# Seven of 392 edge gathers issued row by row on SyncE's queue, and the node-row traffic moved to ScalarE's queue

## The reference

```
xn = layernorm(x)
x  = x + relational_gnn(xn, src, dst, edge_type) + mixer(xn)
x  = x + expert_ffn(layernorm(x))          # top-1 of 32 experts per node
```

## Time and profile before

| | |
|---|---|
| median of the three runs | 785.32 us |
| the profiled execution's own time | 787.59 us |
| its span, first to last instruction | 785.8 us |
| mean granted TensorE clock | 0.904 |
| busy: PE, DVE, POOL, ACT | 76%, 49%, 58%, 21% |
| packets of SP's and ACT's DMA rows, of POOL's | 19236, 22576 |
| edge loop: first and last gather | 47.6 and 630.4 us |

### The profile page before, as it was taken

One profiled execution on the slowest core, in us unless ns is written; L12 is line 12 of the kernel. 1 busy time (PEld: TensorE's weight loads), 2 busy tenths in 40 slices (PEclk: granted clock), 3 DMA queues, 4 the chain that ended last, 5 costly groups with the idle time before them and its releaser, 6 DMA issues.

```text
span 785.8 us, 10435 instructions
## 1 busy us (share of the span) xinstructions
PE 597.3 (76%) x3180; PEld 469.0 (60%) x3181; DVE 386.4 (49%) x1272; ACT 162.6 (21%) x345; POOL 456.2 (58%) x463
## 2 busy tenths in 40 slices
PE   0367776788887884879989899898898894388970
PEld 0356565566665663767667677676676762277850
DVE  3844344333233233445557665666556576823552
ACT  0450000000000000102323222233213253144420
POOL 9146666666666666666666666766666600352264
PEclk9969997799999998699999899999999996579985
DMA  8463333333332334333344343344333416552021
GB/s 228 157 186 85 91 92 87 90 94 86 90 91 85 94 88 134 110 93 110 113 127 121 108 128 114 109 126 118 115 111 111 127 55 204 136 165 74 30 87 51
DMA packets 41872, 86.78 MB, mean 110 GB/s; under 512 B 11280, under 2 KB 23378, under 8 KB 41491
## 3 DMA queue, kind: packets, MB, share of 16 engines
q0 software_dynamic: 22576, 61.01, 26.7%
q1 hardware_dynamic: 18372, 22.95, 9.5%
q10 hardware_dynamic: 864, 2.08, 1.1%
HBM read 73.21 MB, written 12.80 MB: 109 GB/s over the span
## 4 chain that ended last, share of the span: by engine, by line
PE 38%; issue 18%; DVE 15%; another core or an unknown queue 9%; POOL 7%; DMA 6%; ACT 4%; SPq 1%; DVEq 1%; ACTq 0%; POOLq 0%
PE ps L797 18%; PE ps L845 6%; POOL gath L545 6%; DMA gath<-xn_d,src_i 3%; PE ps L1043 3%; PE ps L1052 3%; DVE wmat L1180 2%; DVE acc_raw L1207 2%; DMA both<-in_x 2%; PE ps L814 2%; PE ps L834 2%; PE ps L868 1%; DMA both<-rows_d,inv_i 1%; ACT L658 1%
## 5 line engine op out<-in xcount | busy, mean ns | idle before, releaser
L545 POOL DMA_INDIRECT gath<-xn_d,src_i x392 | 384.7, 981 | 223.7 <-issue 87.6
L797 PE MATMUL ps<-wmat,gath 128*128 128x144 f32 x1568 | 267.9, 311 | 48.1 <-DVE wmat L1180 16.1
L797 PEld LDWEIGHTS ps<-wmat,gath 128*128 128x128 f32 x1568 | 227.9, 202 | 86.4 <-issue 31.3
L1207 DVE TENSOR_TENSOR acc_raw<-acc_raw,ps 128x144 f32 x392 | 101.1, 299 | 286.2 <-PE ps L797 164.4
L1180 DVE TENSOR_TENSOR wmat<-hit,wts 128x576 f32<-128x576 f32 x100 | 75.1, 751 | 0.3
L572 POOL DMA_INDIRECT both<-rows_d,inv_i x25 | 24.3, 973 | 59.0 <-DVE inv_i L1455 46.1
L845 PE MATMUL ps<-wq_wv,acc_raw 128*128 128x256 f32 (+1 forms) x200 | 52.8, 386 | 3.1 <-issue 3.1
L845 PE MATMUL ps<-wk_et,acc_raw 128*128 128x256 f32 (+1 forms) x200 | 54.3, 397 | 0.9 <-issue 0.7
L1501 DVE SCALAR_TENSOR_TENSOR acc_raw<-ps,wts,acc_raw 128x256 f32 x56 | 27.0, 482 | 49.9 <-PE ps L1052 37.3
L834 PE MATMUL ps<-cmat,both 128*128 128x512 f32 (+1 forms) x100 | 47.3, 595 | 3.3 <-issue 3.1
L577 POOL DMA_INDIRECT out<-acc_raw,inv_i x25 | 25.3, 1011 | 39.2 <-DVE acc_raw L1492 33.4
(11 more groups left out here) (196 smaller groups left out, 632.3 us busy)
## 6 DMA issues: line engine op xcount, KB each, us to landing
gath<-xn_d,src_i POOLq DMA_INDIRECT x392
rows_d<-both SPq DMA_DIRECT2D x24, 256.0 KB
both<-in_x SPq DMA_DIRECT2D x24, 128.0 KB
both<-in_x SPq DMA_DIRECT2D x4, 640.0 KB, 16.7
xn_d<-both SPq DMA_DIRECT2D x4, 640.0 KB
acc_raw<-in_w_t SPq DMA_DIRECT2D x1, 2080.0 KB
acc_raw<-in_w_t SPq DMA_DIRECT2D x1, 2048.0 KB, 7.5
acc_raw<-in_type_rows ACTq DMA_DIRECT2D x1, 1600.0 KB, 15.6
```

Source lines behind the costliest of these rows:

```text
L545: g.indirect_dma_start(gath[:, k, :], None, xn_d, bass.IndirectOffsetOnAxis(ap=src_i[:, OCT * q + k:OCT * q + k + 1], axis=0)).then_inc(ga ...
L797: ins = t_.matmul(ps_edge[quarter][:, m * B * WIN:(m + 1) * B * WIN], gath[:, k, m * P:(m + 1) * P], wmat[:, k, :, :].rearrange("p b w -> ...
L1207: d.tensor_tensor(place, place, ps_edge[w][:, m * B * WIN:(m + 1) * B * WIN].rearrange("p (b w) -> p b w", w=WIN), ALU.add).then_inc(added, 1)
```

## The change

1. In octets 6, 13, 20, 27, 34, 41 and 47 the gather of k = 7 leaves POOL. SP brings its 128 rows with 128 DMAs of one row each into a new double buffer `by_row` (2 x 1 KB for each partition). SP first loads the 128 indices into `row_src`, by one small DMA, and reads them eight at a time into registers. From the third one on it waits until the octet that used the same half of `by_row` is through.
2. Column 391, the padding, is not gathered any more; PE multiplies what lies in the buffer by weights of zero.
3. `load_x` and `store_row` of tiles 0 to 20 (loads 0 to 23) move to ACT's queue, behind `keep_x2nt`, and so do both loads of the basis. SP keeps the load of tile 24 and the stores of tiles 21 to 24.
4. The 25 semaphores `f_in` become 13, one for two tiles, each waited for to 32.

```
+BY_ROWS = [6, 13, 20, 27, 34, 41, 47]
+RB = 8
...
+def pool_gathers(q, k):
+    return q + 1 - (sum(o <= q for o in BY_ROWS) if k == OCT - 1 else 0)
...
+        by_row = sb("by_row", [P, 2, D])
+        row_src = sb("row_src", [1, 2, P], I32)
...
 @block.sync
-            sp.wait_ge(keyed, NT)
-            sp.wait_ge(summed, NT)
-            load_basis(0)
-            for t in range(3):
-                load_x(sp, t, once)
-            sp.wait_ge(s_turned, 1)
-            sp.wait_ge(lam_mult, 1)
-            load_basis(1)
-            for t in range(NT):
+            def load_sources(j):
+                c = OCT * BY_ROWS[j] + OCT - 1
+                sp.dma_start(row_src[0:1, j % 2, :], src_rows[c:c + 1, :]).then_inc(row_src_in, 16)
+
+            sp.wait_ge(xn_stored, 16 * (GROUPS + 1))
+            load_sources(0)
+            for j, q in enumerate(BY_ROWS):
+                sp.wait_ge(row_src_in, 16 * (j + 1))
+                if j + 1 < len(BY_ROWS):
+                    load_sources(j + 1)
+                if j >= 2:
+                    sp.wait_ge(multiplied, OCT * (BY_ROWS[j - 2] + 2))
+                for r in range(0, P, RB):
+                    nodes = row_values(sp, row_src[0:1, j % 2, r:r + RB], N - 1, A_SOURCE)
+                    for p in range(RB):
+                        sp.dma_start(by_row[r + p:r + p + 1, j % 2, :], xn_d[ds(nodes[p], 1), :]).then_inc(row_in[j % 2], 16)
+
+            for t in range(INLINE - 2, NT):
+                if t == INLINE - 2:
+                    load_x(sp, NT - 1, once)
                 if t == NT - 1:
                     sp.wait_ge(once.pre_done, NT)
                     load_first(sp, ffn_loaded)
                 store_row(sp, t, once)
-                if t + 3 < NT:
-                    load_x(sp, t + 3, once)
...
 @block.gpsimd, octet
                 for k in range(OCT):
+                    if k == OCT - 1 and q in BY_ROWS or OCT * q + k >= -(-E // P):
+                        continue
                     pool.wait_ge(multiplied, OCT * q + k + 1)
...
 @block.scalar, octet
                     if q - 2 in STEP:
                         keep_x2nt(STEP[q - 2], once)
+                        store_row(act, STEP[q - 2], once)
+                        load_x(act, STEP[q - 2] + 3, once)
...
                 elif beside == "small_a":
+                    act.wait_ge(keyed, NT)
+                    act.wait_ge(summed, NT)
+                    load_basis(0)
+                    for t in range(3):
+                        load_x(act, t, once)
                     act.wait_ge(s_turned, 2)
...
                 elif beside == "small_c":
+                    act.wait_ge(lam_mult, 1)
+                    load_basis(1)
                     act.wait_ge(m_mult, 1)
...
 @block.tensor, edges
-                        if m == 0:
-                            pe.wait_ge(gathered[k], 16 * q + 16)
+                        rows_in = gath[:, k, m * P:(m + 1) * P]
+                        if k == OCT - 1 and q in BY_ROWS:
+                            j = BY_ROWS.index(q)
+                            rows_in = by_row[:, j % 2, m * P:(m + 1) * P]
+                            if m == 0:
+                                pe.wait_ge(row_in[j % 2], 16 * P * (j // 2 + 1))
+                        elif m == 0 and OCT * q + k < -(-E // P):
+                            pe.wait_ge(gathered[k], 16 * pool_gathers(q, k))
...
 @block.tensor, turn_tiles
-                        pe.wait_ge(f_in[t], 16)
+                        if t % 2 == 0:
+                            pe.wait_ge(f_in[t // 2], 16 * min(2, NT - t))
```

More of the change, by code:

```diff
@@ L57 @@
 CLAMPED = "the pairs' experts and tiles are counts from zero, cut to the last expert and tile by a minimum before they are stored"
+A_SOURCE = "the sources of the edges are node numbers, and those of the padding are zero"
 A_NODE = "each base is the least node number among its edges, and acc has a row's width of columns beyond the last node"
@@ L60 @@
 assert STARTS[0] == CHAIN0 and len(STEP) == INLINE and INLINE == NT - 2 and STARTS[-1] == NOCT - 1
+assert BY_ROWS[-1] < NOCT and all(b - a > 1 for a, b in zip(BY_ROWS, BY_ROWS[1:]))
 assert NPAIR % FT == 0 and NPAIR <= P
@@ L101, in mark, with gps_layer @@
         return self.at
-def gps_layer(nc, x, src_t, type_rows, dst_t, dst_rows, basis, comp, loop_w, h_bias, ln_gamma, ln_beta,
+def pool_gathers(q, k):
+    return q + 1 - (sum(o <= q for o in BY_ROWS) if k == OCT - 1 else 0)
+def gps_layer(nc, x, src_t, src_rows, type_rows, dst_t, dst_rows, basis, comp, loop_w, h_bias, ln_gamma, ln_beta,
               w_qk, b_qk, w_v, b_v, bn_gamma, bn_beta, router_w, router_b, w1_t, b1_t, w2_t, relation_of,
@@ L255, in gps_layer @@
         gathered = [sem(f"gathered{k}") for k in range(OCT)]
+        row_src_in = sem("row_src_in")
+        row_in = [sem(f"row_in{j}") for j in range(2)]
         multiplied = sem("multiplied")
@@ L322, in gps_layer @@
         w2_loaded = sem("w2_loaded")
-        f_in = [sem(f"f_in{s}") for s in range(NT)]
+        f_in = [sem(f"f_in{j}") for j in range(PAIRS + 1)]
         f_turned = sem("f_turned")
@@ L481, in _ @@
                     sp.dma_start(dst, frm.rearrange("(k p) -> p k", p=P)).then_inc(weights_loaded, 16)
-            def load_basis(m):
-                sp.dma_start(basis_sb[m], basis[:, m * P:(m + 1) * P, :].rearrange("b p f -> p b f")).then_inc(basis_loaded[m], 16)
-            sp.wait_ge(keyed, NT)
-            sp.wait_ge(summed, NT)
-            load_basis(0)
-            for t in range(3):
-                load_x(sp, t, once)
-            sp.wait_ge(s_turned, 1)
-            sp.wait_ge(lam_mult, 1)
-            load_basis(1)
-            for t in range(NT):
+            def load_sources(j):
[16 more added lines that the diff above has]
+                    load_x(sp, NT - 1, once)
                 if t == NT - 1:
@@ L572, in _ @@
                 g.indirect_dma_start(token[0:n, t, 0:2 * D], None, rows_d,
-                                     bass.IndirectOffsetOnAxis(ap=inv_i[0:n, t:t + 1], axis=0)).then_inc(f_in[t], 16)
+                                     bass.IndirectOffsetOnAxis(ap=inv_i[0:n, t:t + 1], axis=0)).then_inc(f_in[t // 2], 16)
             for t in range(NT):
@@ L618, in _, with load_basis @@
             s.copy(rwt[:, :, :], ps_sum[0][:, 0:KD * X].rearrange("p (k e) -> p k e", k=KD)).then_inc(rwt_ready, 1)
+            def load_basis(m):
+                act.dma_start(basis_sb[m], basis[:, m * P:(m + 1) * P, :].rearrange("b p f -> p b f")).then_inc(basis_loaded[m], 16)
             def octet(q, beside, i):
@@ L794, in edges @@
                     for k in pair:
-                        if m == 0:
-                            pe.wait_ge(gathered[k], 16 * q + 16)
-                        ins = t_.matmul(ps_edge[quarter][:, m * B * WIN:(m + 1) * B * WIN], gath[:, k, m * P:(m + 1) * P],
+                        rows_in = gath[:, k, m * P:(m + 1) * P]
[6 more added lines that the diff above has]
+                            pe.wait_ge(gathered[k], 16 * pool_gathers(q, k))
+                        ins = t_.matmul(ps_edge[quarter][:, m * B * WIN:(m + 1) * B * WIN], rows_in,
                                         wmat[:, k, :, :].rearrange("p b w -> p (b w)"), start=k == pair[0], stop=k == pair[-1])
@@ L1490, in finish @@
                     place = f_ys[0:n, t * D:(t + 1) * D]
-                    v.wait_ge(f_in[t], 16)
+                    v.wait_ge(f_in[t // 2], 16 * min(2, NT - t // 2 * 2))
                     d.tensor_tensor(place, place, token[0:n, t, D:2 * D], ALU.add).then_inc(f_rows, 1)
@@ L1552, in _ @@
                 rank_and_experts(again.own)
-_INS = ["x", "src_t", "type_rows", "dst_t", "dst_rows", "L0_gnn_basis", "L0_gnn_comp", "L0_gnn_loop_w", "L0_gnn_h_bias",
+_INS = ["x", "src_t", "src_rows", "type_rows", "dst_t", "dst_rows", "L0_gnn_basis", "L0_gnn_comp", "L0_gnn_loop_w", "L0_gnn_h_bias",
         "L0_gnn_ln_gamma", "L0_gnn_ln_beta", "L0_mix_W_qk", "L0_mix_b_qk", "L0_mix_W_v", "L0_mix_b_v", "L0_mix_gamma",
@@ L1575, in lay_out @@
     arrays["src_t"] = np.ascontiguousarray(src.T)
+    arrays["src_rows"] = np.ascontiguousarray(src)
     arrays["type_rows"] = np.ascontiguousarray(types)
```

## The result

Over the runs of both kernels the time went from 784.45 to **878.6 us** (872.1 to 885.86): a ratio of 1.119, interval 1.115 to 1.123. That is far outside the range of 775 to 806 us, on the side of the rival in which SP becomes the pace. The profiled execution of the changed kernel took 872.1 us, that of the kernel before 787.59. Ratios here go by the fast executions alone; two slow ones matter, the changed kernel's 885.86 us and the traced one of e12 (874.61 us).

The account below looks back on a forecast made before the run. POOL's gather issues and the k = 7 landing were taken to bound the quiet stages, not the chain. From 787.59 us, -3.75 + 0 + 0 gave 783.8, on the median's scale 781.6, stated as 782 us; range 775 to 806.

Parts of the forecast that it names:

- SP becomes the pace: Rival for the edge loop: rows issued at 0.66 us each on SP make PE wait, 806 us in all; chance 0.18.
- A row on SP, 0.51 us: Price of issuing one row on SP: DMA, register operation and share of the index load, together 0.51 us.
- the bounds I counted on, 0.43 and 0.66: Low and high price in us of one row's issue on SP, taken from other DMAs' issue times.
- threshold (0.637 us): Price of a row from which SP's 896 rows would pace the whole edge loop up to octet 47.
- a reserve of 14% for octet 6 and of 25% for the whole loop: Room above 0.51 us a row before SP's rows come late: limits 0.58 us (octet 6) and 0.637 us (edge loop).
- base_row's 0.28 us: Issue time of a single-row DMA of 0.8 KB on SP, taken as nearest price for a row's DMA.
- hb_col's 0.84 the far end: Furthest issue time among SP's DMAs, which would make a row 1.07 us; not the high end counted on.
- A gather off POOL: 1.25 us in the quiet stages, 0 in the chain: Gain per gather: octets 6, 13, 20 give 3.75 us together; those in the chain (octets 24 to 48) 0.
- PE waits only 1.3 us for gathers, so POOL has room: Chain, 345 to 630 us: PE waits 1.3 us in 285 for gathers, so fewer gathers there gain 0.
- the second rival: POOL's pace counts everywhere, chain included: all eight gathers are worth 1.25 us each, 775.3 us; chance 0.15.
- Contention 0 to 1 us: DMA side of the row transfers: 0 taken, at most 0.05 us on each landing, 1 us over twenty octets.
- ACT's moves and the pairs of `f_in`, 0: Node rows and basis on ACT's queue, and f_in in pairs: cost 0 (up to 17.6 and 1 us).

Follow-up runs that it names:

- e12: e7 with rows of 64 bytes instead of 1024; 871.55 us, ratio 1.106 to the kernel before.
- e6: Changed kernel, but from octet 2 on POOL issues no gathers and only counts up a semaphore; 690.51 us, one run.
- e11: Changed kernel, but from octet 2 on POOL issues a plain DMA of 128 adjacent rows for each indirect gather; 693.58 us, one run.
- e3: Kernel before, with the k = 7 gather left out in twelve quiet-stage octets (2 to 5, 12 to 19); 756.12 us, ratio 0.977.
- e4: Kernel before, with the k = 7 gather left out in the twelve odd chain octets from 25 to 47; 758.28 us, ratio 0.982.
- e2: Changed kernel, with rows on SP for octets 9, 18, 27, 36 and 45 alone; 776.86 us, ratio 1.006 to the kernel before.
- e1: Changed kernel without rows on SP: POOL gathers all but the padding, the other parts stay; 770.73 us, ratio 0.997 to the kernel before.
- e7: Changed kernel, but POOL makes all 392 gathers and nobody waits for the rows SP still brings; 855.54 us, ratio 1.109 to the kernel before.
- e5: Changed kernel, but SP's 896 row DMAs read fixed addresses, without index loads or register operations; 773.31 us, one run.
- e10: Changed kernel, but from octet 2 on POOL's gathers fetch 64 bytes an index instead of 1024; 885.70 us, one run.
- e9: Changed kernel, with rows on SP for octets 9 and 18 alone, 256 rows; 782.91 us, ratio 1.002 to the kernel before.

## Why the prediction was wrong

*A row on SP, 0.51 us: the step that failed.* The value is right for SP by itself (0.514 in e6 and e11, by partly other parts: 0.23 for the DMA instead of 0.28, 0.78 instead of 0.68 for eight indices, and a MOVE). It is wrong beside indirect gathers, where a row costs 0.69 to 0.82 us. Both ends of the bounds I counted on, 0.43 and 0.66, lay below. With the measured price the rival's own arithmetic holds: rows from 52 to 709.6 us, 2.8 us to land, 712.4 instead of 625.5, so 785.3 + 86.9 = 872 us, against 878.6 measured and 872.1 in the profiled execution. Mechanism and threshold (0.637 us) of "SP becomes the pace" were right; its price, 0.66, was 0.074 short, and that is worth 66 us over 896 rows. The sum had a cliff beside it, and I gave a reserve of 14% for octet 6 and of 25% for the whole loop, on an operation that no row priced.

*The sign that was in the trace before.* I took base_row's 0.28 us at 25.8 us, before the first gather, and called hb_col's 0.84 the far end. SP's timeline there:

```profile
46.07 0.94 SPq L481 DMA_DIRECT2D qk_col<-in_L_mix_b_qk  x2
47.05 0.47 SPq L481 DMA_DIRECT2D bn_col<-in_L_mix_gamma  x1
47.57 0.47 SPq L481 DMA_DIRECT2D bn_col<-in_L_mix_beta  x1
48.08 0.59 SPq L481 DMA_DIRECT2D hb_col<-in_L_gnn_h_bias  x1
```

Six DMAs of the same line, back to back: the first four take 0.43 to 0.47 us, and the two that start after POOL's first gather (47.6) take 0.59 and 0.84. The only other burst beside gathers before the change is of four DMAs at 298 us, and the first load of x in it took 0.51 us instead of 0.43. From 368 us on, 20 stores and 20 loads stand in pairs, one pair about every 12 us. They took 0.33 and 0.43, which is why I thought these undisturbed prices. They are, but not for a stream. Three long DMAs out of the six in these bursts are a hint, not more.

*A gather off POOL: 1.25 us in the quiet stages, 0 in the chain.* Measured 1.34 (e3) and 1.16 (e4). The rule "PE waits only 1.3 us for gathers, so POOL has room" was wrong. POOL's 2 us of stalls per octet are there in both stages; in the first I had counted the issues into the loop in spite of them, and in the chain I called them room. A gather less still shortens the octet. That was the second rival, and e4 bears out its value (by which way the waits go back to POOL is not shown), though the change could not cash it.

*Contention 0 to 1 us: wrong.* e2 lost 6 us against e1 where it should have won 5 x 1.2, and e7's gather loop, in one trace, some 12 us to rows that nobody used. Eight gathers fewer are worth 10 us at best. So this change would not have paid even if every row had come in time, on a version as e2; only the rows at fixed addresses (e5, 773.31 beside 771.41, one run) come near to even.

*ACT's moves and the pairs of `f_in`, 0: right* (e1). *The rows overlap: right*, 0.51 us apart where one in series would take 2.75. (The fit of 2.0 us for a DMA that the prediction takes from the Trainium skill is given there, in "DMA: Bandwidth & Descriptors", Anatomy of one DMA, for DMAs that GpSimd issues; these are SP's.) The chances of a slower result add up to 0.20, not 0.21.

"DMA: Bandwidth & Descriptors" of the Trainium skill (Rules for kernel authors) says that spreading DMAs over the issuing engines only saves the sequencer's issue time. The trace agrees with the rule and shows its other side: issue time was all that moved, 1.25 us on POOL against 128 x 0.73 = 94 us on SP. As for the 600 ns that the same page of the Trainium skill gives as the floor of a register load (Latency and other measured facts): DVE's took 0.34 us for four, and SP's 0.78 for eight, 0.10 a row, where that page's figure had given the dearer estimate of 0.15.

*Open.* What SP and POOL share is not shown. The stops hit any instruction of a stream, do not depend on the bytes of either side (e10, e12), and the instructions behind one pass at once; a supply of instructions that falls behind would look like this, and so would a shared path that the gathers' descriptors take. No run tells these apart. One thing the pages do say: the packets that bring instructions are 82 in the changed kernel and 60 in the one before, so a stop, of which there are 460, is not one such packet. Nor is it settled where the 12 us of e7 lie: 3.6 until octet 7, 5.7 in octets 21 to 24, 3.4 from octet 25 on. Those four octets took between 47.0 and 53.4 us from kernel to kernel without a cause that I could name (51.6 in the kernel before), and octets 1 to 6, with 11.87 us in e7 and 11.41 in e1, took 11.80 in the kernel before, without rows.

## What to carry to other kernels

Price an issue from rows that stand beside the same neighbours and in the same density as it will: a stream of small DMAs beside indirect gathers cost 0.73 us each where the same stream alone cost 0.51. Count instructions as well as DMAs, for here each kind was stopped. In a loop of engines that wait for each other in turn, a stall isn't room: leave out one piece of work in some rounds and measure what comes back, before anything is built to take it over.

## What the runs showed of the hardware

- Beside POOL's indirect gathers (0.95 us each, one in 1.25 us) SP's sequencer, when it issues a stream, stops for 0.70 us at about every fourth to sixth instruction, be it a register operation, a MOVE or a DMA (0.16 stops per instruction in e5, 0.17 in the changed kernel, 0.24 in e9). Beside plain DMAs issued by POOL it doesn't (18 stops in 2688 instructions of e11, all beside its 16 indirect gathers).
- A plain DMA of 128 rows costs POOL 0.54 us (e11), the indirect one 0.95, with 64 bytes a row (e10) or 1 KB.
- One row at an address from a register costs SP 0.41 us undisturbed (e6, e11), at a fixed address beside gathers 0.33 (e5); the load of eight registers 0.78 (e11).
